# PEER retrieval on one core: two mask products in succession, one of them in the score banks, then four groups of expert rows

## The reference, cut to what matters

```python
sim1 = einsum('bthd,hkd->bthk', q[..., 0, :], keys[:, :, 0, :])
sim2 = einsum('bthd,hkd->bthk', q[..., 1, :], keys[:, :, 1, :])
s1, i1 = top_k(sim1, K); s2, i2 = top_k(sim2, K)
fs, pk = top_k(all_sc, K)                 # best 8 of the 64 sums, 8 heads
fi = take_along_axis(all_idx, pk, axis=-1)
hidden = gelu(einsum('btd,bthkd->bthk', xn, expert_down[fi]))
hidden = hidden * relu(fs)
out = einsum('bthk,bthkd->btd', hidden, expert_up[fi])
```

## Time and profile before

| what | value |
|---|---|
| median of 3 runs | 2035.67 us (2034.08 to 2035.78) |
| the profiled execution: its own time | 2040.18 us |
| the profiled execution: its span | 2038.5 us |
| TensorE busy | 87% of the span |
| VectorE busy | 49% |
| mean granted TensorE clock | 0.925 of full speed |
| instruction fetches of queue q8 | 102 packets, 1.67 MB |

### The profile page before, as it was taken

The page is one execution under the profiler, slowest core; times in us unless marked ns, Lnnn a source line. Parts: engine busy times, 40 slices in busy tenths (PEclk is TensorE's granted clock), DMA queues, the critical chain, the costliest instruction groups (busy, mean ns, idle before and its releaser), DMA issues. The chain is left out here.

```text
span 2038.5 us, 31919 instructions
## 1 busy us (share of the span) xinstructions
PE 1765.7 (87%) x13350; PEld 1097.5 (54%) x13350; DVE 1006.4 (49%) x2506; ACT 356.6 (17%) x591; POOL 316.3 (16%) x139
## 2 busy tenths in 40 slices
PE   5878899999999998789999979999596008999998
PEld 2346678888888887644444434444242003478543
DVE  1228896877868763023111111111238993265676
ACT  2222102111011020010111111111134522202200
POOL 0001314224133152004400000000035000003000
PEclk9988899999999997789999989999798559999899
DMA  6000000000000000113000040000100000440000
GB/s 288 31 0 6 2 1 8 8 2 9 7 3 8 1 8 7 59 70 124 0 0 0 0 186 0 0 0 0 62 0 0 0 0 6 166 165 1 6 16 21
DMA packets 11978, 64.93 MB, mean 32 GB/s; under 512 B 2634, under 2 KB 7234, under 8 KB 8002
## 3 DMA queue, kind: packets, MB, share of 16 engines
q1 hardware_dynamic: 11842, 62.98, 7.9%
HBM read 60.87 MB, written 2.10 MB: 31 GB/s over the span
## 5 line engine op out<-in xcount | busy, mean ns | idle before, releaser
L563 POOL TENSOR_TENSOR peer_bm<-peer_bm,peer_slots 128x512 f32<-128x512 f32 x64 | 193.8, 3028 | 609.8 <-DVE peer_bm L650 609.8
L436 PE MATMUL peer_ps_h<-all_x,layer_down 128*128 128x256 f32 (+1 forms) x1024 | 241.4, 389 | 0.0
L474 PE MATMUL peer_ps_o<-peer_hg,layer_up 128*128 128x256 f32 x1024 | 227.3, 382 | 1.3 <-DVE peer_hg L682 1.3
L474 PEld LDWEIGHTS peer_ps_o<-peer_hg,layer_up 128*128 128x128 f32 x1024 | 196.1, 192 | 33.5 <-issue 5.3
L436 PEld LDWEIGHTS peer_ps_h<-all_x,layer_down 128*128 128x128 f32 x1024 | 192.4, 193 | 28.5 <-issue 1.9
L1058 DVE SCALAR_TENSOR_TENSOR skills_hid<-skills_ps_u,all_pair_w,skills_act_g 128x512 f32<-128x512 f32 x64 | 47.9, 749 | 286.0 <-PE skills_ps_u L1019 286.0
L451 PE MATMUL peer_ps_w<-peer_bm,peer_am 64*64 64x32 f32 x8192 | 145.9, 228 | 27.7 <-DVE peer_hg L682 22.2
L451 PEld LDWEIGHTS peer_ps_w<-peer_bm,peer_am 64*64 64x64 f32 x8192 | 138.4, 145 | 48.0 <-issue 47.9
L1252 PE MATMUL quant_ps_m<-quant_gate,layer_qw 128*128 128x512 f32 x96 | 43.0, 610 | 125.5 <-DVE quant_gate L1132 125.5
L652 DVE TENSOR_TENSOR peer_am<-all_iota_a,peer_slots 128x2048 f32<-128x2048 f32 x64 | 146.2, 2285 | 0.0
L508 ACT ACTIVATE peer_hg<-peer_ps_h 128x512 f32<-128x512 f32 x128 | 76.5, 597 | 369.7 <-PE peer_ps_h L436 369.7
(11 more groups left out here) (279 smaller groups left out, 2332.7 us busy)
## 6 DMA issues: line engine op xcount, KB each, us to landing
layer_w<-in_l_w SPq DMA_DIRECT2D x16, 1024.0 KB, 6.0
layer_skill<-in_skills SPq DMA_DIRECT2D x2, 3072.0 KB, 10.1
skills_w<-in_skills SPq DMA_DIRECT2D x2, 3072.0 KB, 13.0
skills_w<-in_skill_shared SPq DMA_DIRECT2D x2, 3072.0 KB, 20.5
layer_down<-in_down SPq DMA_DIRECT2D x1, 4096.0 KB, 24.3
layer_up<-in_up SPq DMA_DIRECT2D x1, 4096.0 KB, 33.5
swiglu_w<-in_cond SPq DMA_DIRECT2D x2, 1541.0 KB, 8.2
layer_q<-in_q_w SPq DMA_DIRECT2D x1, 2304.0 KB, 15.2
```

Of the source, the lines that this page charges most:

```text
L436: mm = pe.matmul(ps_h[group % 2][:, r, :], down[:, c, j * P:(j + 1) * P], g.x[:, c, bass.ds(i * PB, PB)], start=(c == 0), stop=(c == C - 1))
L474: mm = pe.matmul(ps_o[:, c, :], up[:, j, c * P:(c + 1) * P], hg[half][:, j, :], start=(j == 0), stop=(j == NJ - 1))
L563: pool.tensor_tensor(bm[c % RING][:], bm[c % RING][:], slots[half][:, 2, c * PAIRS:(c + 1) * PAIRS].unsqueeze(2).to_broadcast([P, PAIRS, WJ]),
```

## The change

A helper `product(c, first)` gives the place of a mask: the banks of `ps_s` for an odd chunk of every block but block 0, `ps_w` otherwise. `weigh` writes there and L682 reads from there. An even chunk after the first and an odd chunk after 1 wait for the product two chunks back (`p_done` n in place of n + 1); chunk 0 keeps its old wait; chunk 1 waits for `sim_read`, that is until the picks have read the scores. In all blocks but block 0 the expert rows come after each odd chunk, four groups at once. At the block's end the wait for the last product now stands ahead of `scores(i + 2, 0)`, since the scores take over the banks.

```diff
+        spare = ps_s[:].rearrange("p z (m j) -> p z m j", j=WJ)
+
+        def product(c, first):
+            return spare if c % 2 and not first else ps_w[:]
...
-            def weigh(i, c):
+            def weigh(i, c, first, route):
                 n = i * CHUNKS + c
+                to = product(c, first)
                 pe.wait_ge(a_done, n + 1)
                 pe.wait_ge(b_done, n + 1)
-                pe.wait_ge(p_done, n + 1)
+                if first or c == 0:
+                    pe.wait_ge(p_done, n + 1)
+                elif c == 1:
+                    pe.wait_ge(sim_read, (i + 2) * PT if route else NPB * PT)
+                else:
+                    pe.wait_ge(p_done, n)
...
-                            mm = pe.matmul(ps_w[of, z, m, :], am[c % RING][token, m, of], bm[c % RING][token, m, :],
+                            mm = pe.matmul(to[of, z, m, :], am[c % RING][token, m, of], bm[c % RING][token, m, :],
...
-                    weigh(i, c)
-                    if more:
+                    weigh(i, c, first, route)
+                    if more and (first or c % 2):
                         if first and c % CPT == 0:
                             scores(i + 1, c // CPT)
-                        for group in range(c * GPC, (c + 1) * GPC):
+                        for group in range((c if first else c - 1) * GPC, (c + 1) * GPC):
...
+                pe.wait_ge(p_done, i * CHUNKS + CHUNKS + 1)
                 if route:
                     scores(i + 2, 0)
-                pe.wait_ge(p_done, i * CHUNKS + CHUNKS + 1)
...
-                    dve.tensor_tensor(acts, ps_w[:].rearrange("p z m j -> p z j m"), acts, ALU.mult).then_inc(p_done, 1)
+                    dve.tensor_tensor(acts, product(c, first).rearrange("p z m j -> p z j m"), acts, ALU.mult).then_inc(p_done, 1)
```

## The result

The changed kernel takes 2059.95 us in the median of 4 runs (2058.05 to 2062.04), against 2035.72 us (2034.08 to 2041.98, 4 runs) for the kernel before: a ratio of 1.0113, with a 95% interval of 1.0089 to 1.0138. It is 24 us slower, where 8 us faster was forecast, and outside the range of 2017 to 2040 us.

The account below looks back on a forecast made before the run. TensorE's instruction stream was taken to bound blocks 1 to 6, with waits and a 0.62 clock in block 7. Terms -6.7 - 1.2 - 9.1 + 8.9 = -8.1 us gave a median of 2027.6 us, range 2017 to 2040.

Parts of the forecast that it names:

- Term 4: Blocks 1 to 6: paired products use up instructions faster than they are fetched; loss of 0.37 us a pair, +8.9 us.
- rival B: Blocks 1 to 6: each pair stalls in full for instructions, losing 28.8 us, sum +11.8, 2047.5 us; chance 0.15.
- a third of the bound: Blocks 1 to 6: fetch loss taken as 0.37 us of at most 1.2 us a pair, queued instructions covering some.
- The scores start where they did: Block's end: moving the wait ahead of the scores costs nothing, the last L682 being over some 3.5 us before.
- Term 1: Blocks 1 to 6: paired products need one switch to 64x64 tiles instead of two; 24 places at 0.28 us, -6.7 us.
- Term 2: Loop's jump in blocks 1 to 6: chunk 1's product no longer waits for L682 of chunk 0; -1.2 us.
- Term 3: Block 7: products and L682 wait less for each other, so the output begins at 813.8 instead of 822.89; -9.1 us.
- Rival A: Blocks 1 to 6: a deep queue hides the instruction fetches; -17.0 us, 2018.7 us; chance 0.20.
- C: Block 7 gives little, held back by fetches or clock: 3 us remain of 9.1; -2, 2033.7 us; chance 0.08.
- D: Some blocks: the third chunk's product waits about 1 us for VectorE after late picks; -4, 2031.7 us; chance 0.07.
- The signs that were named: Blocks 1 to 6: over 485 us means fetches fully exposed; idle "issue" in mid-product or a second product over 2.0 us.

Follow-up runs that it names:

- the first experiment: Against the changed kernel, the old order and block 0's scores ahead of the wait came back, banks and looser waits kept; 2027.68 us, ratio 0.995 to the kernel before.

## Why the prediction was wrong

**Term 4 was mis-sized, and it decided.** The mechanism was named, and rival B had the sign; the size taken was 0.37 us a pair, +8.9 in all. The profile has 24.8 us of idle "issue" in blocks 1 to 6 against 1.5 before, 23.3 more, and 6.7 us of lower clock behind it. With the gain of the switches and of the jump put back, the loss is 26.7 + 5.0 + 1.2 = 32.9 us, 1.37 us a pair; the 2.9 us that idle and clock leave over fit stops that cost a little more than the idle time shown. Three things went wrong in that step. The pace of a starved stream was read off one pair of fetches at the jump as 3.2 us; block 7 of the changed kernel has 3.6 to 4.0. So the bound of 1.2 us a pair was no bound; by the same reckoning it is 1.6 to 2.0. Then "a third of the bound" rested on two fetches within 4.5 us without a stall; but one piece per 2.25 us is more than such a pair needs to show, since it may hold one fetch interval of over 3.6 us, and that says nothing on 2.0 us. And what idle time does to the clock was weighed in block 7 alone.

**"The scores start where they did" failed in block 0** (+5.0 us). The paragraph on costs of nothing named the work that covers the moved wait for the steady blocks, four groups that take some 7 us. Block 0 keeps one product and two groups, VectorE does a piece of a pick ahead of its multiplication there, and the 3.6 us of scores had been the cover. The edit is in shared code; the block with another order had to be walked through as well. The run that undoes it brings block 0 back to 110.4 us, the run that does it alone to the old kernel takes it to 115.5.

**Term 1, the switches,** was right in kind. A pair without a stop in block 3 takes 11.09 us, from 505.21 to 516.30, against 2 x 5.65 = 11.30 before: 0.21 us a pair and 5.0 in all, where 6.7 was taken.

**Term 2, the jump,** came as said: no wait for VectorE in blocks 1 to 6.

**Term 3, block 7,** forecast -9.1 and measured -8.0 (29.4 us), and -7.4 (30.0 us) where it is done alone, with -8.1 in the time. The chain was VectorE's at first, as laid out: its first five multiplications there start 3.9 us apart. The last three follow at 3.2 to 3.6 us and wait for TensorE's products, which run at the lower clock as the prediction assumed.

**Rival A** fell. So did, for this stream, the rule of the Trainium skill (Runtime: NRT & Kernel Launch, Instruction fetch mechanics) that fetching is hidden: with 256 instructions in 2.0 us it is not. **Rival B,** given 0.15, was the case, and it had been priced at 2047.5 us; most of the other 12 are the clock (6.7) and block 0 (5.0). The prediction says that its range, 2017 to 2040, leaves out the far end of B; it leaves out B's own price, and with it nearly all of a rival that had been given 0.15. **C and D** did not happen.

**The signs that were named** for fetches exposed in full are the ones that came: blocks 1 to 6 above 485 us, and rows of the second product with idle "issue" in their middle.

**The better version** is the first experiment: old order, both pairs of banks, block 0 untouched. It is 10 us below the kernel before, and by the two ratios some 33 us below the changed one.

## What to carry to other kernels

Count instructions, not only columns: in this kernel a stretch of small matmuls at 8 ns an instruction used up a fetched piece of 256 in 2.0 us, and the next one took 3.6 us or more; slow work between two such stretches is what hides the fetches, and putting them side by side takes it away. A second buffer and a new order are two changes: here the buffers alone gain 10 us, and with the order the kernel loses 24. When shared code is reordered, look for the cover of each moved wait in every variant of the loop, the first and last block above all.

## What the runs showed of the hardware

- The mask product's time followed the number of its loads and matmuls: the same columns with half of them took 1.09 us instead of 2.00.
- A starved TensorE got a piece of 256 instructions (the size by the grid of the stops) every 3.6 to 4.0 us in block 7, and went on 2.2 to 2.9 us after a fetch was seen to start, at 23 stops of blocks 1 to 6.
- Stops of 1.2 to 1.7 us in a stretch that is otherwise busy were followed by expert rows at the lower clock in four of the 24 pairs, 1.7 us each; other stops of that length were not. With the wide tiles in pairs the clock fell with no stop ahead of it (0.65 in the second product).
- Loads of 64 rows by 128 columns ran at 57 ns each in the stream, against 15 ns for 64 by 64, both at full clock: the wide tile costs nearly four times the narrow one.
